# Graph attention with gathered rows: 14 instead of 10 tiles fetched row by row, in longer and split portions per group

## The reference

```python
Q_h, K_h, V_h = x @ Wq + bq, x @ Wk + bk, x @ Wv + bv      # per node, (N, 8, 12)
E = edge_attr @ We + be                                     # per edge
score = K_h[src] * Q_h[dst] / sqrt(12) * E
score = exp(clip(score.sum(-1), -5.0, 5.0))                 # per edge and head
wV = segment_sum(V_h[src] * score, dst)
Z  = segment_sum(score, dst)
out = layernorm(x + (wV / (Z + 1e-6)).reshape(N, 96))
```

## Time and profile before

| what | value |
|---|---|
| median of 3 runs | 993.1 us |
| the profiled execution, its own time | 993.86 us |
| its span, first to last instruction | 992.1 us |
| POOL busy | 737.3 us, 74% |
| DVE busy | 653.0 us, 66% |
| PE busy | 643.3 us, 65% |
| ACT busy | 189.4 us, 19% |
| granted TensorE clock, mean | 0.807 |

### The profile page before, as it was taken

How to read it: one execution, slowest core, us unless ns; L and a number is a source line. 1 busy time by engine, 2 the same in 40 slices (tenths; PEclk the granted TensorE clock), 3 DMA queues, 4 the chain that set the end, 5 groups by cost and what they waited for, 6 DMA issues and landing times. The chain is left out here.

```text
span 992.1 us, 15976 instructions
## 1 busy us (share of the span) xinstructions
PE 643.3 (65%) x3276; PEld 419.8 (42%) x3276; DVE 653.0 (66%) x1307; ACT 189.4 (19%) x378; POOL 737.3 (74%) x778
## 2 busy tenths in 40 slices
PE   6778777766566766666557656664675566657563
PEld 5655555444343434344334434443343344334342
DVE  6638987877666675766566656664775566657655
ACT  4842211111111111111111111111111111111111
POOL 7777777777777777777777777777777777777772
PEclk9888988788877777778777877788788878777876
DMA  6999776666655557656565665565665655664531
GB/s 201 311 285 241 185 188 184 188 173 172 176 147 168 150 140 185 165 138 175 143 173 150 164 177 149 139 177 145 168 170 145 180 147 137 177 176 123 145 80 47
DMA packets 103482, 165.77 MB, mean 167 GB/s; under 512 B 46285, under 2 KB 66126, under 8 KB 103375
## 3 DMA queue, kind: packets, MB, share of 16 engines
q1 hardware_dynamic: 64399, 84.88, 31.3%
q0 software_dynamic: 36544, 74.37, 28.4%
q10 hardware_dynamic: 2432, 5.41, 1.6%
HBM read 152.19 MB, written 12.39 MB: 166 GB/s over the span
## 5 line engine op out<-in xcount | busy, mean ns | idle before, releaser
L424 POOL DMA_INDIRECT kv<-kv_table,idx x740 | 703.7, 951 | 225.6 <-issue 224.3
L527 PE MATMUL psT<-identity,qe 96*128 96x96 f32 x782 | 115.3, 307 | 242.7 <-DVE qe L872 242.6
L955 DVE TENSOR_TENSOR qke<-psT,kv 128x768 f32<-128x768 f32 (+1 forms) x99 | 93.6, 945 | 266.5 <-DMA kv<-kv_table,idx 257.2
L506 PE MATMUL psE<-ea,we 97*96 97x512 f32 x392 | 259.7, 799 | 0.8 <-ACT kv L646 0.8
L527 PEld LDWEIGHTS psT<-identity,qe 96*128 96x128 f32 x782 | 93.2, 178 | 259.8 <-DVE qe L872 259.7
L576 PE MATMUL psA<-place,msg 128*104 128x104 f32 x1536 | 170.1, 266 | 22.4 <-DVE msg L982 22.1
L576 PEld LDWEIGHTS psA<-place,msg 128*104 128x104 f32 x1536 | 160.1, 180 | 51.2 <-DVE msg L982 45.0
L676 ACT ACTIVATE qe<-psE 96x1024 f32<-96x1024 f32 (+1 forms) x99 | 99.8, 1008 | 217.2 <-PE psE L506 217.2
L872 DVE TENSOR_TENSOR qe<-psQ,qe 96x1024 f32<-96x1024 f32 (+1 forms) x99 | 118.4, 1196 | 7.8 <-ACT qe L676 7.8
L506 PEld LDWEIGHTS psE<-ea,we 97*96 97x96 f32 x392 | 75.9, 219 | 80.2 <-issue 80.2
L690 ACT ACTIVATE msg<-clipped 128x64 f32<-128x64 f32 (+1 forms) x99 | 25.3, 255 | 419.8 <-DVE clipped L970 413.8
(11 more groups left out here) (105 smaller groups left out, 349.5 us busy)
## 6 DMA issues: line engine op xcount, KB each, us to landing
ea<-eaT SPq DMA_DIRECT2D x99, 384.0 KB, 4.0
q_parts<-rel_table SPq DMA_DIRECT2D x99, 252.0 KB
kv<-kv_table,idx POOLq DMA_INDIRECT x740
q_full<-kv_table SPq DMA_DIRECT2D x640, 0.8 KB
q_full<-kv_table ACTq DMA_DIRECT2D x640, 0.8 KB
qwin<-q_table SPq DMA_DIRECT2D x198, 23.6 KB
xb<-xrows SPq DMA_DIRECT2D x24, 144.0 KB
out<-ob SPq DMA_DIRECT2D x24, 144.0 KB
```

Of the source, the lines that this page charges most:

```text
L424: pool.indirect_dma_start(kv[:, k, t], None, kv_table, sources).then_inc(kv_in[k], 16)
L506: last = nc.tensor.matmul(psE[0:D, h, 0:size], we[:], ea[:, k % EAR, edge:edge + size], start=True, stop=True)
L527: last = nc.tensor.transpose(psT[:, t % 2, t // 2 * D:(t // 2 + 1) * D], qe[0:D, k % 2, t * P:(t + 1) * P], identity[0:D, 0:D])
L955: nc.vector.tensor_tensor(qke[:, 0:nt].rearrange("p (t b) d -> p b t d", **by_bank), psT[:, :, 0:nt // 2 * D].rearrange("p b (t d) -> p b ...
```

## The change

Three things change.

1. `SP_ROWS` becomes 10 and `ACT_ROWS` 12. A tile takes 13 turns of SP or 11 of ACT. `BY_ROW` grows from 10 tiles to 14: SP fetches the last tiles of groups 18, 31, 44, 57, 70 and 83, ACT those of groups 16, 27, 38, 49, 60, 71, 82 and 93. POOL issues 736 gathers of K and V rows instead of 740.
2. The row numbers are loaded into registers in two portions per turn: 5 and 5 on SP, 6 and 6 on ACT.
3. The load of the window bases on SP no longer asserts that they are in range.

```diff
-SP_ROWS, ACT_ROWS = 8, 8
+SP_ROWS, ACT_ROWS = 10, 12
+SP_STEP, ACT_STEP = 5, 6
-SP_TILES = tuple(22 + SP_TURNS * i for i in range(5))
-ACT_TILES = tuple(23 + ACT_TURNS * i for i in range(5))
+SP_TILES = tuple(18 + SP_TURNS * i for i in range(6))
+ACT_TILES = tuple(16 + ACT_TURNS * i for i in range(8))
...
-        def load_single_rows(eng, i, j, rows):
-
-            count = min(rows, P - j * rows)
-            edge = i * P + j * rows
+        def load_single_rows(eng, i, start, count):
+
+            edge = i * P + start
...
             for p in range(count):
-                eng.dma_start(kv_rows[j * rows + p:j * rows + p + 1, i], kv_table[bass.ds(nodes[p], 1), :]
+                eng.dma_start(kv_rows[start + p:start + p + 1, i], kv_table[bass.ds(nodes[p], 1), :]
...
                 return nc.values_load_multi_w_load_instructions(
-                    qbase_int[0:1, bass.ds(2 * g, 2 * count)], engines=[sp.engine], min_val=0, max_val=NR - QW)[1]
+                    qbase_int[0:1, bass.ds(2 * g, 2 * count)], engines=[sp.engine], min_val=0, max_val=NR - QW,
+                    skip_runtime_bounds_check_because="the lowest target node of half a group, at most N")[1]
...
                         if 0 <= turn < len(SP_TILES) * SP_TURNS:
-                            load_single_rows(sp, turn // SP_TURNS, turn % SP_TURNS, SP_ROWS)
+                            start = turn % SP_TURNS * SP_ROWS
+                            for row in range(start, min(P, start + SP_ROWS), SP_STEP):
+                                load_single_rows(sp, turn // SP_TURNS, row, min(SP_STEP, P - row))
...
                         if first and 0 <= turn < len(ACT_TILES) * ACT_TURNS:
-                            load_single_rows(act, len(SP_TILES) + turn // ACT_TURNS, turn % ACT_TURNS, ACT_ROWS)
+                            start = turn % ACT_TURNS * ACT_ROWS
+                            for row in range(start, min(P, start + ACT_ROWS), ACT_STEP):
+                                load_single_rows(act, len(SP_TILES) + turn // ACT_TURNS, row, min(ACT_STEP, P - row))
```

## The result

The changed kernel takes 1038.2 us (median of 4 runs, 1037.72 to 1038.93) against 993.4 us for the kernel before in the same comparison (992.93 to 994.11): 4.5% slower, ratio 1.0451 [1.0433, 1.0469]. The prediction was 995.7 us with a range of 987.8 to 1003.0. The direction is right, the size is wrong by 42 us.

The account below looks back on a forecast made before the run. POOL's gathers at 1.256 us each, plus any wait POOL is made to take, were held to bound the kernel. -5.0 (four gathers) + 7.6 (wait at group 16) = +2.6 us, from 993.1 to 995.7 us; range 987.8 to 1003.

Parts of the forecast that it names:

- What the change adds on ScalarE: ACT's queue per group: four more rows 1.60 us, second register load 0.74 us, together 2.34 us.
- ACT's round: ACT's path for four groups after the first catching-up: about 37.9 us against POOL's 39.3 on average, so no second stall.
- ScalarE becomes the bound for all of the by-row phase: Rival: one more slow PE product per four groups makes POOL wait again and again; 1005 us, chance 0.14.
- the stop at group 16: POOL's 97th gather waits for group 14's query product, starting at 174.4 instead of 166.8 us: 7.6 us lost.
- 10.9 us of delay: ACT's added time, followed from group 4 to group 11, makes group 14's query product end at 174.1 instead of 163.23.
- the slack: At group 16's first gather: it could have started at 163.5 but starts at 166.8 us, leaving POOL 3.3 us.
- slow PE products: TensorE's clock on the path to group 14: 1.7 us per further slow product, 0 to 3.4 us, only in the range.
- SP's part: On SyncE: two more rows and a second load, 1.5 us per turn, absorbed by its waiting for `q_done`; taken as nothing.
- the assertions: Range assertions removed from SP: a gain between 0 and 5.1 us at the start, taken as 0.
- Four gathers of 1.256 us: On POOL: 736 gathers for 740 take 5.0 us off, fully only while POOL never waits.
- The sentence on issue time: Skill page's claim that issue time is usually small; set against ACT's 3.2 us per group, a third of a group's time.
- Not held up: Rival: group 14's query product stays within POOL's spare time, so only four gathers count; 988.1 us, chance 0.24.

Follow-up runs that it names:

- experiment 1: The changed kernel with each turn's row numbers loaded in one portion (12 on ACT, 10 on SP): 996.4 us, ratio 1.0039.
- experiment 7: The kernel before, still 8 rows and 10 tiles, without range assertions and with ACT's eight row numbers loaded as 4 and 4: 996.4 us, ratio 1.0011.
- experiment 13: The changed kernel with ACT's twelve rows in portions of eight and four: 1001.2 us, ratio 1.0056.
- experiment 3: The changed kernel without POOL's wait for the query product (CLOSE = NG): 1038.9 us, ratio 1.0485.
- experiment 14: The changed kernel with one load per turn (12 on ACT, 10 on SP) and without POOL's wait for the query product: 992.6 us, ratio 0.9971.
- experiment 15: The changed kernel with twelve rows in one load on both SP and ACT, 15 tiles, and without POOL's wait for the query product: 988.5 us, ratio 0.9957.
- experiment 4: The changed kernel with only ACT's part of the change; SP takes 8 rows in one load for five tiles: 1043.3 us, ratio 1.0502.

## Why the prediction was wrong

**The step that failed** is the price of the second register load, under "What the change adds on ScalarE": "0 if it were hidden, 0.74 or somewhat more if not; I take 0.74". It takes 1.63 us (median of 80). The row that I took it from the earlier trace rows is a load of eight registers at a multiple of 32 bytes; the changed kernel's second load starts 24 bytes into a turn. The trace of before had only loads of the first kind, so its rows gave a lower end and not an upper one. "Somewhat more" was no bound, and the range inherited that.

**The size of the addition.** Predicted 2.34 us on ACT per group; the stretch grew by 3.42 us (7.71 - 4.29). The four rows (1.60 us, as predicted) are 1.56 in experiment 1 (4.76 - 3.20); the rest, 1.86, is the second load with the gaps beside it.

**Which case it falls into.** I estimated ACT's round at 37.9 us against 39.3 for POOL, a margin of 1.4 us in four groups. A further 1.1 us in each of four groups is 4.4, part of it in slack, and the margin is gone: the round is 40.6 us. So the rival "ScalarE becomes the bound for all of the by-row phase" took place, to which I gave 0.14, though by another way than its condition (a slow PE product in each four groups). Its price was wrong as well: 0.3 us in each of 19 rounds. ACT's lag against POOL is 40.6 - 39.3 = 1.3 us in a round; over the 19 rounds from group 16 on that is 25 us, which is what POOL's 23 later waits add (24.3), and the stop at group 16 was 17.1 us in place of 7.6. I had computed the margin and said that it grows by 1.4 us; I hadn't asked how little more per group would turn its sign. It was 0.35 us by the prediction's own numbers; the runs put the knee at a stretch of about 7.4 us, which is 0.8 us above the 4.29 + 2.34 that it assumed.

**The stop at group 16 was undersized too.** The prediction's 10.9 us of delay for 2.34 us more in each group are, in proportion, 2.4, 7.0, 9.9 and 15.9 us for what experiments 7, 1 and 13 and the changed kernel added to the stretch (0.51, 1.51, 2.13 and 3.42 us). The query product of group 14 came 5.2, 9.0, 13.3 and 19.3 us later: 2 to 3.4 us more each time. And the slack was 2.5 us and not 3.3, since the gather starts 1.07 us behind the product, in each of these traces. The product in experiment 1, then the gather that waited for it:

```profile
171.67 0.60 PE L519 MATMUL psQ<-q_parts,qwin 126*96 126x512 bf16 x2
```

```profile
173.34 0.94 POOL L427 DMA_INDIRECT kv<-kv_table,idx  x1 [7.67 <-issue]
```

With the load at 0.74 us the stop would therefore have been some 11 us and the time about 999 us (an estimate), inside the range and 3 us above the forecast: experiment 13, whose stretch of 6.42 us is just below the assumed 6.63, stops for 11.1 us and is 0.56% slower. What makes up the 2 to 3.4 us isn't shown; the prediction had set aside 0 to 3.4 us for slow PE products, and no run parts these from the rest.

**Right, by the runs.** The place of POOL's stop (the 97th gather) and its releaser (without the wait for it, in experiment 3, the stop is gone); in experiment 1 also that it comes once. That the stop there is 7.7 us, beside the 7.6 predicted, is luck: it comes from 1.51 us more per group and not from 2.34. SP's part is nothing (0.9991 alone), and the assertions are nothing (0.9994 alone). Four gathers of 1.256 us are taken off POOL; in experiment 14, where nothing else holds it, the others were 4 ns slower each, which no experiment explains.

**The sentence on issue time.** Twelve rows in 4.76 us are 0.40 us of ACT's queue for each DMA of 768 bytes. The page "DMA: Bandwidth & Descriptors" of the Trainium skill, section "Issuing engines are not separate DMA queues", calls issue time usually small beside the DMA. No row here has the time to landing of a single row's DMA, so that sentence isn't tested for one of them; for a queue that issues twelve in a turn it is the issue time that counts: issuing (line 220) is 28% of the chain that ended last after the change, DMA 5%.

**The rivals not taken.** "Not held up" needs a delay within the slack; even eight rows in two loads (experiment 7) stop POOL for 2.6 us, and one load of twelve for 7.7 us. It came true only where POOL's wait was removed together with the second load (experiments 14 and 15).

**Open.** Why ACT's group 4 starts 2.7 us later in experiment 4; the 2 to 3.4 us of delay up to group 14; the 4 ns per gather in experiment 14; the 5.0 us more behind the last gather; and how exactly a load's price follows from its address and size (below).

## What to carry to other kernels

The price of an instruction is read from rows whose operands lie as those of the new one will; where only friendlier ones exist, the upper bound of the range has to be far away, and a load into registers is best kept whole and at a multiple of 16 bytes. Where two engines' rounds differ by a few per cent, work out first at which addition the slower one changes: past that point each microsecond per round is paid in every round. And an engine that issues many small DMAs is judged by its queue in the timeline, never by its busy share.

## What the runs showed of the hardware that I had not expected

The time of a load of registers from SBUF depends on the address of its first value. Medians in us over all loads of one kind in these traces (ACT; for 5 registers SP, in the changed kernel). Bytes are counted from the start of the row numbers; no row shows the address of that start itself:

| registers | first value at a multiple of 16 bytes | elsewhere |
|---|---|---|
| 2 | 0.67 | 0.78; behind a load 0.49 |
| 4 | 0.48; behind DMAs 0.59 | |
| 5 (SP) | 0.57 | 1.32; behind DMAs of the turn 1.35 |
| 6 | 0.93; behind DMAs 1.04 | 1.63; behind a load 1.34 |
| 8 | 0.72 | 1.93 |
| 10 | 1.17 | 2.47 |
| 12 | 0.96 | 2.78 |

In the left column four registers more cost 0.24 us (0.48, 0.72, 0.96). In the right one a single register costs about as much: 0.21 us each from 8 (1.93) to 12 (2.78), and from 6 (1.63) to 10 (2.47). On the left the sizes that aren't multiples of four are dearer than the next larger one (6: 0.93 against 8: 0.72), as if the last two were loaded one by one. That a load goes in pieces of 16 bytes where it can, and value by value elsewhere, fits these numbers, but it is argued from them and not shown by itself.

Where the load stands counts for less: the same unaligned load of six took 1.34 us behind another load and 1.63 behind DMAs, an aligned one of four 0.48 as a turn's first and 0.59 behind DMAs.
